# Expert blocks stored by block number, without zeros for the experts' output area

## The chip, the cores and the metric

One core of a Trainium2 chip runs the whole program. The metric is the device time of one execution in microseconds. TensorE (PE), VectorE (DVE), ScalarE (ACT), GpSimd (POOL) and SyncE (SP) each run their own list of instructions; semaphores order them, and SyncE here issues most of the DMA transfers.

## What is computed

16 images of 128 channels and 32 x 32 points go through six layers, each added to what comes in. Only the fourth is touched, a mixture of eight gated experts, of which each token takes the two best:

```python
x = x + conv0(group_norm(x)); x = x + conv1(group_norm(x))
t = tokens(x)                                   # 16 * 1024 tokens of 128
t = t + attention(layer_norm(t))
# the gated mixture
n = layer_norm(t)
vals, idx = top_k(n @ Wg + bg, 2);  w = softmax(vals)
a, g = split(n @ W1[e] + b1[e], 2)              # for each expert e of 8
y[e] = (silu(a) * g) @ W2[e] + b2[e]
t = t + sum_k w[k] * y[idx[k]]
t = t + decay_attention(layer_norm(t));  t = t + second_mixture(layer_norm(t))
```

## The kernel before, in words

The program runs five stages, one after the other, each a block of its own in which every engine has its list; at a block's end all engines meet before the next begins.

1. `convolution_stage` (L80) does both convolution layers. SyncE loads the images and the small weights, waits for the maps of the attention over space (L202 to L208), and then, from L210, issues `FILLS` = 17 transfers that write zeros over the whole of `slots_out`, and one that writes zeros over the last 8 blocks of `slots_in` (L215). At the stage's end TensorE transposes the images and ScalarE copies them into the tile `T` (L468).
2. `attention_stage` (L557) begins with loads of its weights on SyncE's queue (L739 to L743, counted by the semaphore `loaded`, and eight of `Wo` at L749) and with GpSimd's constants (L791 to L807). VectorE waits for the five loads and all constants, then takes the statistics of the first tokens (L914). TensorE's first work is the transposition of the first normalised tokens (L1160). For each image the stage also picks the two experts of each token. A token's row number in `slots_in` is `e * REGION` plus a count, for each of the two; `slots_of` (L1013) keeps the numbers in `route["slots"]`, 128 x 256, and GpSimd writes the normalised tokens to those rows.
3. `experts_stage` (L1295, here with `gated=True`, names with `c_`) walks `MAX_BLOCKS` = 71 blocks of `SLOTS` = 512 rows. VectorE plans first: from the counts in `route["base"]` come the blocks per expert (`full`), their running sum (`ends`), and for each block number its expert and first row (`row_i`). Every expert has a region of 16,896 rows in `slots_in` and `slots_out`, filled from its start. For a block `j` SyncE loads `row_i[j]` into a register and issues the load of its rows (L1408), and for block `j - 5` loads its row again and issues the store of its results to the same rows of `slots_out` (L1413).
4. `decay_stage` gathers the results back: GpSimd reads row numbers from `route["slots"]` and issues gathers from `slots_out` (L2446 to L2454).
5. `mixture_stage` is the last layer.

The work of the experts stage is an order written out by hand. For a block `j`, VectorE runs, in `@block.vector`:

```python
for j in range(MAX_BLOCKS):
    multiply(j, 0)          # L1502: silu(a) * g, first 128 hidden
    if j + 1 < MAX_BLOCKS:
        split_x(j + 1)      # L1495: x - x_hi, the low part of the input
    low(j)                  # L1508: low part of the product
    if j >= 2:
        copy_y(j - 2)       # L1515: results out of PSUM
    multiply(j, 1)          # L1502: second 128 hidden
```

`multiply(j, u)` waits for ScalarE's `first(j, u)` (L1554). ScalarE runs, in this order, `add_bias(j - 2)`, `high(j - 1, 1)` (L1562, which waits for `multiply(j - 1, 1)`), `first(j, 0)`, `high_x(j + 1)`, `high(j, 0)`, `first(j, 1)`. GpSimd copies a block's weights (L1436) and computes the low part of the second product (L1447) once `high(j, 1)` is done. TensorE begins a block with `unit(j, 0)` (L1610 to L1612), which waits for `split_x(j)`; `second(j - 1, 0)`, `turn_x(j + 1)`, `turn_y(j - 2)`, `unit(j, 1)` and `second(j - 1, 1)` follow.

## Time and profile before

| | |
|---|---|
| median of three runs | 4566.6 us (4561.16 to 4569.98) |
| the profiled execution | 4562.08 us, its span 4560.4 us |
| busy share: PE, DVE, ACT, POOL | 82%, 72%, 47%, 42% |
| moved by DMA | 237.52 MB, of it written to HBM 144.31 MB |
| experts stage, blocks | 71, stored by 71 transfers of 256 KB |
| zero fills | 17 of 4096 KB (`slots_out`), one of 2048 KB and eight of 256 KB (`slots_in`) |

Times in the profile are microseconds from the start of the span. A row of a timeline gives the start, the length, the engine, the line of the kernel, the operation and its tiles, the count of merged instructions and, in brackets, how long the engine was idle before and what released it. SPq is SyncE's instruction queue: the length of a DMA row there is the time to issue it, not to move the data. PEclk is the granted clock of TensorE, 1.00 for 2.4 GHz and 0.50 for 1.2 GHz.

### The profile page before, as it was taken

How to read it: one execution, taken by the hardware profiler on the slowest of the kernel's cores; microseconds unless marked ns; L12 is line 12 of the kernel's file. 1: busy time of each engine (PE TensorE's matmuls, PEld its weight loads, DVE VectorE, ACT ScalarE, POOL GpSimd, SP SyncE). 2: the span in 40 equal slices, each digit the busy share in tenths (PEclk: the TensorE clock that was granted, in tenths of full speed). 3: DMA queues.
4: the chain of work that ended last, by engine and by line, in shares of the span. 5: the costliest groups of instructions: out<-in, count | busy, mean ns of one | idle time of the engine just before them, and what ended most of it. 6: DMA issues, size and time to landing. Idle time of an engine off the chain costs nothing. (4 is left out here: it accounts for less than half of the span.)

```text
span 4560.4 us, 74420 instructions
## 1 busy us (share of the span) xinstructions
PE 3719.4 (82%) x21802; PEld 1983.8 (44%) x21802; DVE 3278.3 (72%) x6678; ACT 2140.1 (47%) x3740; POOL 1924.8 (42%) x2046
## 2 busy tenths in 40 slices
PE   1627999989999898999947994488888786999999
PEld 0111222332333332333216883255555555777777
DVE  6737788888888888888815664555556566777777
ACT  1012666666666666666636773122222233444444
POOL 0311033322223323332234553466666653777776
PEclk9976999999999999999978997699999998999999
DMA  2982111121122222222003331000000001000000
GB/s 74 353 302 39 24 30 35 30 37 32 34 36 37 38 37 38 37 37 37 11 23 121 105 105 53 16 30 29 28 28 28 28 19 33 24 23 23 23 23 23
DMA packets 132977, 237.52 MB, mean 52 GB/s; under 512 B 27632, under 2 KB 32952, under 8 KB 132600
## 3 DMA queue, kind: packets, MB, share of 16 engines
q1 hardware_dynamic: 115736, 200.51, 16.4%
q0 software_dynamic: 16384, 33.59, 2.5%
q8 instruction: 134, 2.20, 0.2%
q14 instruction: 147, 1.20, 0.1%
q10 hardware_dynamic: 576, 0.02, 0.0%
HBM read 89.74 MB, written 144.31 MB: 51 GB/s over the span
## 5 line engine op out<-in xcount | busy, mean ns | idle before, releaser
L1143 ACT ACTIVATE b_probs<-b_ps_s 128x512 f32<-128x512 f32 x2048 | 1173.8, 596 | 708.1 <-PE b_ps_s L1187 670.0
L940 DVE TENSOR_REDUCE b_maxes<-b_ps_m 128x1 f32<-128x1024 f32 x1024 | 1215.6, 1214 | 268.7 <-PE b_ps_m L1175 266.0
L1187 PE MATMUL b_ps_s<-b_qs,b_ks 99*128 99x512 bf16 x2048 | 788.9, 390 | 54.8 <-DMA b_ks<-b_k_parts 15.2
L1175 PE MATMUL b_ps_m<-b_ks,b_qs 96*128 96x512 bf16 x2048 | 642.5, 396 | 113.5 <-DVE b_maxes L940 92.0
L1881 POOL TENSOR_TENSOR e_act_lo<-e_act,e_act_hi 128x512 fp32r<-128x512 f32 x384 | 521.8, 1359 | 239.4 <-DVE e_act_hi L1810 239.4
L1199 PE MATMUL b_ps_o<-b_probs,b_vs 128*32 128x512 f32 x4096 | 559.6, 619 | 23.6 <-ACT b_probs L1143 22.8
L1187 PEld LDWEIGHTS b_ps_s<-b_qs,b_ks 99*128 99x128 bf16 x2048 | 199.3, 98 | 845.6 <-ACT b_probs L1143 668.8
L2082 ACT ACTIVATE e_act<-e_ps_h,e_bias 128x512 f32<-128x512 f32 x384 | 264.3, 689 | 411.6 <-PE e_ps_h L2136 290.9
L1985 DVE TENSOR_TENSOR e_act<-e_act,e_ps_g 128x512 f32<-128x512 f32 x384 | 261.5, 681 | 145.9 <-ACT e_act L2082 145.9
L814 POOL TENSOR_TENSOR b_rstd<-b_mv,b_eps 128x8 f32<-128x8 f32 x32 | 6.5, 202 | 744.5 <-DVE b_mv L921 744.5
L1175 PEld LDWEIGHTS b_ps_m<-b_ks,b_qs 96*128 96x128 bf16 x2048 | 188.7, 100 | 301.5 <-DVE b_maxes L940 179.3
L2669 DVE TENSOR_TENSOR d_inner<-d_ps_s,d_decay 128x512 f32<-128x512 f32 x256 | 169.1, 681 | 180.6 <-PE d_ps_s L2951 176.9
L880 POOL DMA_INDIRECT slots_in<-b_xn,b_slot x256 | 248.1, 969 | 97.6 <-issue 81.0
L2450 POOL DMA_INDIRECT d_y<-slots_out,d_slot_now x256 | 247.2, 966 | 88.0 <-issue 71.5
L1810 DVE CAST e_act_hi<-e_act 128x512 fp32r<-128x512 f32 x384 | 244.2, 636 | 0.0
L2134 PE MATMUL e_ps_h<-e_x_hi,e_w_hi 128*128 128x512 f32 x384 | 159.0, 414 | 47.4 <-DVE e_x_lo L1969 42.5
L2826 ACT ACTIVATE d_xn<-tokens,d_shift,d_rstd 128x128 f32 (+1 forms) x256 | 104.9, 482 | 181.4 <-POOL d_shift L2503 181.4
L1502 DVE SCALAR_TENSOR_TENSOR c_act<-c_ps_h,c_bias,c_half_way 128x512 f32<-128x512 f32 x142 | 106.6, 751 | 103.5 <-ACT c_half_way L1554 100.5
L1199 PEld LDWEIGHTS b_ps_o<-b_probs,b_vs 128*32 128x32 f32 x4096 | 81.7, 109 | 206.0 <-issue 141.9
L2685 DVE TENSOR_TENSOR d_state<-d_ps_k,d_block_mask 128x128 f32<-128x128 f32 x224 | 64.2, 287 | 142.4 <-PE d_ps_k L2977 140.6
L853 POOL TENSOR_TENSOR b_taken<-b_hit 128x64 bf16<-128x64 f32 x16 | 5.2, 324 | 380.2 <-DVE b_hit L1001 380.2
L2863 ACT ACTIVATE d_o_chan<-d_ps_o 128x512 f32<-128x512 f32 x64 | 38.2, 597 | 257.8 <-PE d_ps_o L2985 257.8
(434 smaller groups left out, 7415.9 us busy)
## 6 DMA issues: line engine op xcount, KB each, us to landing
slots_out<-nothing SPq DMA_DIRECT2D x17, 4096.0 KB, 29.8
b_qs<-b_q_parts SPq DMA_DIRECT2D x96, 256.0 KB, 9.1
c_xin<-slots_in SPq DMA_DIRECT2D x71, 256.0 KB, 2.6
slots_out<-c_y_out SPq DMA_DIRECT2D x71, 256.0 KB, 2.0
b_q_parts<-b_qparts SPq DMA_DIRECT2D x16, 768.0 KB, 3.6
a_x<-in_x_dram SPq DMA_DIRECT2D x8, 1024.0 KB, 10.2
normalised_t<-d_xT SPq DMA_DIRECT2D x16, 512.0 KB
e_xb<-normalised_t SPq DMA_DIRECT2D x32, 256.0 KB, 2.8
```

Source lines behind the costliest of these rows:

```text
L880: nc.gpsimd.indirect_dma_start(out=slots_in, out_offset=bass.IndirectOffsetOnAxis(ap=slot[:, k * TILES + j:k * TILES + j + 1], axis=0), in ...
L940: nc.vector.tensor_reduce(maxes[:, kv, u:u + 1], ps_m[:, u % 2], AX.X, ALU.max).then_inc(m_free, 1)
L1143: nc.scalar.activation(probs[:, s % PROBS, j * HALF:(j + 1) * HALF], ps_s[:, j % 2], ACT.Exp).then_inc(exp_done, 1)
L1175: last = nc.tensor.matmul(ps_m[:, u % 2, half * HALF:(half + 1) * HALF], qs[0:STACK, buffer, h * PX + qt * P:h * PX + qt * P + P], ks[0:ST ...
L1187: nc.tensor.matmul(ps_s[:, j % 2], ks[0:rows, parity, kv * PX + tt * P:kv * PX + tt * P + P], qs[0:rows, parity, h * PX + half * HALF:h * ...
L1199: last = nc.tensor.matmul(ps_o[32 * j:32 * j + 32, :], vs[:, parity, tt, g // 2, :], probs[:, s % PROBS, j * HALF:(j + 1) * HALF], start=( ...
L1810: copy(act_hi[:, u % ring_a], act_buf[:, u % RING]).then_inc(hi_done, 1)
L1881: nc.gpsimd.tensor_tensor(act_lo[:, u % ring_a], act_buf[:, u % RING], act_hi[:, u % ring_a], ALU.subtract).then_inc(lo_done, 1)
L1985: nc.vector.tensor_tensor(act_buf[:, u % RING], act_buf[:, u % RING], ps_g[:, (u // units_of_gate) % 2], ALU.mult).then_inc(weighed, 1)
L2082: nc.scalar.activation(act_buf[:, u % RING], ps_h[:, u % ring_h, 0], ACT.Gelu, bias=bias[:, bias_column(u, 0)]).then_inc(a_ready, 1)
L2450: nc.gpsimd.indirect_dma_start(out=y[:, i // TILES, i % TILES], out_offset=None, in_=slots_out, in_offset=bass.IndirectOffsetOnAxis(ap=slo ...
L2669: tt(inner[:, c].rearrange("p (j l) -> p j l", j=GH), ps_s[:, :, c * P:(c + 1) * P], decay[:, g * GH:(g + 1) * GH], ALU.mult).then_inc(inn ...
```

## The change

A block's results are stored at the block's number times 512 rows instead of at the rows that its tokens came from. `slots_out` shrinks from 139,264 rows to 36,352, all of which the 71 stores write, and the 17 fills go. Since the row numbers in `route["slots"]` are numbers in `slots_in`, VectorE shifts them for the gather. For each expert, `moved` is the distance from its region's start to its blocks' place, and `jump` the difference of one expert's to the one before; the numbers of expert 0 stay as they are, and seven passes over the 256 columns add `jump[e]` to all numbers from `e * REGION` on. These passes are spread over blocks 8 to 16.

```diff
-            some = FILL_BLOCKS * SLOTS
-            for k in range(FILLS):
-                sp.dma_start(slots_out[k * some:(k + 1) * some].rearrange("(p b t) c -> p b (t c)", p=P, b=FILL_BLOCKS),
-                             nothing[:].rearrange("p (a n) -> p a n", a=1).broadcast_to([P, FILL_BLOCKS, SLOTS])
-                             ).then_inc(cleared, 16)
...
+        moved = sb(pre + "_moved", [P, E])
+        jump = sb(pre + "_jump", [P, E])
+        placed = past[:].rearrange("p j e -> p (j e)")[:, 0:IMAGES * 2 * TILES]
+        beyond = begun[:].rearrange("p j e -> p (j e)")[:, 0:IMAGES * 2 * TILES]
...
-            sp.wait_ge(cleared, 16 * (FILLS + 1))
+            sp.wait_ge(cleared, 16)
...
-                    at = sp.value_load(row_i[0:1, done:done + 1], min_val=0, max_val=SLOT_ROWS - SLOTS)
-                    sp.dma_start(slot_rows(slots_out, at), y_out[:, done % 2]).then_inc(y_sent[done % 2], 16)
+                    sp.dma_start(slot_rows(slots_out, done * SLOTS), y_out[:, done % 2]).then_inc(y_sent[done % 2], 16)
...
+            steps = [0]
+
+            def renumber(ins):
+
+                steps[0] += 1
+                ins.then_inc(renumbered, 1)
+                dve.wait_ge(renumbered, steps[0])
+
+            def block_starts():
+
+                renumber(tt(moved[:], ends[:], full[:], ALU.subtract))
+                renumber(nc.vector.scalar_tensor_tensor(moved[:], moved[:], float(SLOTS), regions[:], ALU.mult,
+                                                        ALU.subtract))
+                renumber(tt(jump[:, 1:E], moved[:, 1:E], moved[:, 0:E - 1], ALU.subtract))
+                renumber(nc.vector.tensor_copy(placed, route["slots"][:]))
+
+            def move_from(e):
+
+                renumber(nc.vector.scalar_tensor_tensor(
+                    beyond, route["slots"][:], float(e * REGION),
+                    jump[:, e:e + 1].broadcast_to([P, IMAGES * 2 * TILES]), ALU.is_ge, ALU.mult))
+                renumber(tt(placed, placed, beyond, ALU.add))
+
             split_x(0)
             for j in range(MAX_BLOCKS):
                 multiply(j, 0)
+                if j == E:
+                    block_starts()
+                if E < j < 2 * E:
+                    move_from(j - E)
+                if j == 2 * E:
+                    nc.vector.tensor_copy(route["slots"][:], placed)
                 if j + 1 < MAX_BLOCKS:
                     split_x(j + 1)
...
-        slots_out = nc.dram_tensor("slots_out", (SLOT_ROWS, C), F32, kind="Internal").ap()
+        slots_out = nc.dram_tensor("slots_out", (MAX_BLOCKS * SLOTS, C), F32, kind="Internal").ap()
```

Three places show how instructions move. The first is SyncE at the end of the convolution stage and the start of the attention stage, before the change:

```order
L207 DMA a_rows<-a_map 32x16x32 x2
L212 DMA slots_out<-nothing 2048x1x512 x17
L215 DMA slots_in<-nothing 1024x1x512
L83 UNCONDITIONAL_BRANCH
L737 UNCONDITIONAL_BRANCH
L739 DMA b_wq<-in_L_attn_Wq_dram 128x128
```

and with it (here and below its own line numbers, which are smaller by 2 to 7 up to L1323, and differ again behind):

```order
L205 DMA a_rows<-a_map 32x16x32 x2
L208 DMA slots_in<-nothing 1024x1x512
L81 UNCONDITIONAL_BRANCH
L730 UNCONDITIONAL_BRANCH
L732 DMA b_wq<-in_L_attn_Wq_dram 128x128
```

The fill of `slots_in` and all loads of the next stage now stand directly behind the loads of `a_rows`. The second place is VectorE in the experts stage, around block 8 and the first half of block 9, with the change; before it the rows L1524 to L1528 and the pass of block 9 are not there, and all others stand in the same order:

```order
L1499 SCALAR_TENSOR_TENSOR c_act<-c_ps_h,c_bias,c_half_way 128x512 x2
L1524 TENSOR_TENSOR c_moved<-c_ends,c_full 128x8
L1525 SCALAR_TENSOR_TENSOR c_moved<-c_moved,c_regions 128x8
L1527 TENSOR_TENSOR c_jump<-c_moved 128x7
L1528 CAST c_past<-route_slots 128x256
L1492 TENSOR_TENSOR c_x_lo<-c_ps_x,c_x_hi 128x512
L1505 TENSOR_TENSOR c_act_lo<-c_act,c_act_hi 128x512
L1512 COPY c_y_out<-c_ps_t 128x512
L1499 SCALAR_TENSOR_TENSOR c_act<-c_ps_h,c_bias,c_half_way 128x512 x2
L1532 SCALAR_TENSOR_TENSOR c_begun<-route_slots,c_jump 128x256
L1535 TENSOR_TENSOR c_past<-c_past,c_begun 128x256
```

The two `c_act` products in a row are `multiply(j - 1, 1)` and `multiply(j, 0)`; the new work is behind the second, ahead of `split_x(j + 1)`. The third place is SyncE in the steady part of the experts stage, one load and one store before:

```order
L1407 TENSOR_LOAD c_row_i
L1407 ISA x2
L1408 ISA
L1408 DMA c_xin<-slots_in 128x512
L1412 TENSOR_LOAD c_row_i
L1412 ISA x2
L1413 ISA
L1413 DMA slots_out<-c_y_out 128x512
```

and with the change:

```order
L1405 TENSOR_LOAD c_row_i
L1405 ISA x2
L1406 ISA
L1406 DMA c_xin<-slots_in 128x512
L1410 DMA slots_out<-c_y_out 128x512
```

The store's register load is gone. The lists of TensorE, ScalarE and GpSimd hold the same instructions in the same order as before.

## Rows read from the trace of the kernel before

**Rows 1.** The page: what the DMA engines moved, in 40 equal slices.

```profile
GB/s 74 353 302 39 24 30 35 30 37 32 34 36 37 38 37 38 37 37 37 11 23 121 105 105 53 16 30 29 28 28 28 28 19 33 24 23 23 23 23 23
```

**Rows 2.** Timeline from 288 to 326 us, all engines (start, length, what).

```profile
288.68 1.08 ACT L468 ACTIVATE tokens<-a_ps_big 128x512 f32 x2 [0.41 <-PE a_ps_big L523]
291.62 10.81 SPq L215 DMA_DIRECT2D slots_in<-nothing  x1
303.74 4.18 SPq L739 DMA_DIRECT2D b_wq<-in_L_attn_Wq_dram  x1
303.75 0.31 POOL L791 MEMSET b_wo<- 128x256 f32 x1 [56.69 <-POOLq L55]
...
309.34 0.29 POOL L807 TENSOR_SCALAR_AFFINE_SELECT b_tri<-b_ones 128x128 bf16<-128x128 bf16 x1
...
311.84 1.24 SPq L743 DMA_DIRECT2D b_bg<-in_L_ffn_bg_dram  x1
...
316.90 1.65 DVE L914 BATCH_NORM_STATS2 b_stats<-tokens 128x6 f32<-128x128 f32 x8 [42.04 <-DMA b_bg<-in_L_ffn_bg_dram]
...
325.23 1.09 PE L1160 MATMUL b_ps_x<-ident,b_xn 128*128 128x128 f32 x4 [36.24 <-POOL b_xn L837]
```

**Rows 3.** Line L1394, the experts' weights of 64 KB: issue (ns) and landing.

```profile
L1394 SPq DMA_DIRECT2D c_w_raw<-in_L_ffn_W_dram x16: 424/432/452, 2390.9 to 2412.8; - x16
...
DMA to landing us min/median/max: 2.3/2.8/3.1
```

**Rows 4.** Windows: length, PE busy, (other engines,) PEclk, DMA share, GB/s.

```profile
2440.00:2780.00 340.00, 340.00 (x1740) 1.00 0.31 103
...
320.00:346.00 26.00, 13.41 (x32) 6.06 (x32) 4.42 (x8) 3.56 (x6) 10.35 (x10) 0.50 0.11 36
...
275.00:290.00 15.00, 10.10 (x77) 7.92 (x75) 0.00 (x0) 10.85 (x20) 0.00 (x0) 1.00 1.03 384
```

**Rows 5.** Timeline of one block of the experts stage, 2443 to 2449 us.

```profile
2443.66 0.75 DVE L1502 SCALAR_TENSOR_TENSOR c_act<-c_ps_h,c_bias,c_half_way 128x512 f32<-128x512 f32 x1 [1.35 <-ACT c_half_way L1554]
...
2444.00 1.30 POOL L1447 TENSOR_TENSOR c_act_lo<-c_act,c_act_hi 128x512 fp32r<-128x512 f32 x1
...
2444.69 0.69 DVE L1495 TENSOR_TENSOR c_x_lo<-c_ps_x,c_x_hi 128x512 fp32r<-128x512 f32 x1 [0.28 <-ACT c_x_hi L1547]
...
2445.30 0.68 DVE L1508 TENSOR_TENSOR c_act_lo<-c_act,c_act_hi 128x512 fp32r<-128x512 f32 x1
...
2445.90 0.68 DVE L1515 COPY c_y_out<-c_ps_t 128x512 f32<-128x512 f32 x1
...
2446.41 0.39 PE L1610 MATMUL c_ps_h<-c_x_hi,c_w_now 128*128 128x512 f32 x1
...
2446.63 0.75 DVE L1502 SCALAR_TENSOR_TENSOR c_act<-c_ps_h,c_bias,c_half_way 128x512 f32<-128x512 f32 x1
...
2447.41 0.62 ACT L1562 CAST c_act_hi<-c_act 128x512 fp32r<-128x512 f32 x1
...
2448.74 0.75 DVE L1502 SCALAR_TENSOR_TENSOR c_act<-c_ps_h,c_bias,c_half_way 128x512 f32<-128x512 f32 x1 [1.36 <-ACT c_half_way L1554]
```

**Rows 6.** Timeline, VectorE's operations nearest to the new ones, two stretches.

```profile
2392.31 1.32 DVE L1473 TENSOR_TENSOR c_ends<-c_ends,c_full 128x1 f32<-128x1 f32 x7
...
247.93 0.42 DVE L399 TENSOR_TENSOR a_pyr<-a_pyr,a_shift 128x256 f32<-128x256 f32 x1
...
249.54 0.29 DVE L409 TENSOR_SCALAR a_pyr<-a_tmp 128x256 f32<-128x256 f32 x1
```

**Rows 7.** Timeline of the convolution stage, VectorE beside GpSimd.

```profile
141.31 1.25 POOL L265 TENSOR_TENSOR a_x<-a_x,a_kept 128x512 f32 x1 [0.73 <-DVE a_kept L371]
...
141.93 1.18 DVE L371 SCALAR_TENSOR_TENSOR a_kept<-a_product,a_spikes 128x512 f32<-128x512 f32 x1 [0.21 <-DVE a_product L365]
```

**Rows 8.** Timeline of the experts stage's end.

```profile
2786.90 0.69 DVE L1515 COPY c_y_out<-c_ps_t 128x512 f32<-128x512 f32 x1 [3.25 <-PE c_ps_t L1631]
...
2788.32 0.33 SPq L1413 DMA_DIRECT2D slots_out<-c_y_out  x1
```

More of the change, by code:

```diff
@@ L28 @@
 SPARE_BLOCKS = E
-FILL_BLOCKS = 16
-FILLS = (E * REGION // SLOTS + SPARE_BLOCKS) // FILL_BLOCKS
 SLOT_ROWS = E * REGION + SPARE_BLOCKS * SLOTS
@@ L77, with convolution_stage @@
 SQUEEZED = 8
-def convolution_stage(nc, T, ident, slots_in, slots_out, nothing, cleared, dram):
+def convolution_stage(nc, T, ident, slots_in, nothing, cleared, dram):
     with ExitStack() as ctx:
@@ L1352, in experts_stage @@
         plan = sem(pre + "_plan")
+        renumbered = sem(pre + "_renumbered")
         padded = sem(pre + "_padded")
@@ L3055, in _ @@
                 pool.wait_ge(ident_zero, 2)
-        convolution_stage(nc, T, ident, slots_in, slots_out, nothing, cleared, dram)
+        convolution_stage(nc, T, ident, slots_in, nothing, cleared, dram)
         gates = sb("gates", [P, TILES * IMAGES * E])
```

## The prediction

> **What bounds the kernel now.** I read the page by 40 slices first. In slices 2 and 3 the DMA engines move 353 and 302 GB/s, ten times what they move through most of the rest [rows 1]: these are the 17 zero fills that the change removes, 4096 KB each. So the first question is whether anything waited for them. The list of waits around the end of the convolution stage says that VectorE did, 42.0 us until the load of `b_bg` landed, and that GpSimd waited 56.7 us for its release at the stage's end [rows 2].
>
> The timeline of that stretch shows the order of events [rows 2]. ScalarE's last work of the convolution ends at 288.68 + 1.08 = 289.76. SyncE is then still issuing: the last fill of `slots_out` holds it until 291.62 and the fill of `slots_in`, which comes behind, until 302.43. Only then does the stage end for all; GpSimd starts at 303.75, 1.32 us later. The loads of the attention stage stand behind the fills in the same queue: the issue of `b_wq` takes 4.18 us and that of the fifth load 1.24, and VectorE, which waits for all five, starts at 316.90. The nearest issues in a queue with little in it, weights of the experts, take 0.43 us and land in 2.3 to 3.1 us [rows 3]. Before 289.76 the list of waits has no engine that waits for a fill.
>
> The other end of the change lies in the experts stage. There TensorE is busy 340.00 of 340.00 us, at a granted clock of 1.00 [rows 4], one block every 5.08 us (the DVE row L1502 of `multiply(j, 0)` comes at 2443.66 and 2448.74 [rows 5]). VectorE works about two thirds of that time, and idles 1.36 us just before `multiply(j, 0)` and 0.28 before `split_x` [rows 5].
>
> **The fills removed.** SyncE now reaches the 2048 KB fill of `slots_in` some 165 us before the stage's end. So ScalarE ends the stage: 289.76 + 1.32 = 291.08 is GpSimd's start. Two things must then be ready for VectorE. GpSimd's constants take from 303.75 to 309.34 + 0.29 = 309.63, that is 5.88 us, so they are ready at 296.96. SyncE's five loads take 5 x 0.43 = 2.2 us to issue and up to 3.1 to land, ready at 296.4. The constants are the later by a little; with 0.1 for the semaphore VectorE starts at 297.1 and not at 316.90: **19.8 us earlier**, and all behind it moves as one piece. The eight `b_wo` loads behind the five are issued by some 4 us later, before 298, and TensorE wants them at its first transposes, 325.23 - 19.8 = 305.4 [rows 2]: hidden. `slots_out` needs no zeros for anyone else: a gathered row is always one that a block stored.
>
> **VectorE's new work in the experts stage.** 19 instructions, all between `multiply(j, 0)` and `split_x(j + 1)`, each but the last waited for before the next: in block 8 three on 8 columns and a cast of 256; in blocks 9 to 15 two on 128x256; in block 16 a cast of 256. Prices [rows 6]: seven linked operations on one column take 1.32, so 0.20 each with the wait; 128x256 with two inputs in SBUF 0.42; 256 columns with one input in SBUF 0.29. I take 0.42 + 0.03 for each of the large ones, the cast among them, so 0.90 for a pair; 0.29 + 0.03 is the lower bound.
>
> Does 0.90 fit in? The idle time says so (1.36 + 0.28 = 1.64 a block), but the order does not. From one `multiply(j, 0)` to the next runs a chain without TensorE, by the durations and starts in rows 5: `multiply(j, 0)` 0.75, `split_x` 0.61, `low` 0.60, `copy_y` 0.68, from `multiply(j, 1)` to ScalarE's `high(j, 1)` 0.78, from there over `first(j + 1, 0)` to `multiply(j + 1, 0)` 1.33. That is 4.75, under TensorE's 5.08; with the pair it is 5.65, so each of seven blocks goes 0.57 us slower than TensorE could: 4.0 us. It shows as TensorE waiting for `x_lo` at the start of a block.
>
> Block 8 comes first, and there the lag that TensorE can bear counts. `x_lo` is ready at 2444.69 + 0.69 = 2445.38 and used at 2446.41: 1.03 to spare [rows 5]. The inserted work would start at 2444.41, while GpSimd's L1447, which reads two tiles in SBUF, runs from 2444.00 to 2445.30. Such a meeting is in the trace: beside L265, VectorE's L371, of 512 columns with two inputs in SBUF, takes 1.18, where L1508 of that kind and size takes 0.68 alone, and it ends 0.55 after L265 does [rows 5, 7]. So the first small operation gets going at 2445.30, the cast ends at 2445.30 + 3 x 0.20 + 0.45 = 2446.35, `split_x` at 2447.04, and TensorE loses 0.63. Without the meeting `x_lo` would come at 2446.15 and leave 0.26 to spare: the stage would lose 4.0 - 0.26 = 3.7 and not 4.6. From block 9 on the two stay apart: `high(j - 1, 1)` ends 0.71 before `multiply(j, 0)` starts and releases L1447, whose 1.30 end at +0.59, and the pair starts at +0.75.
>
> The Trainium skill (SBUF — State Buffer, section Who interferes with whom) says of this meeting that a VectorE instruction with two SBUF inputs and a GpSimd instruction that reads SBUF take a shared port in turn, the later one fully blocked; the trace agrees, with the 1.18 beside 0.68. With that rule in block 8 the stage loses 4.6, without it 3.7; if it struck in all of blocks 9 to 15 too, the upper bound below would hold.
>
> In block 16 the cast makes the chain 5.20: 0.1. **Together 4.7 us lost**, between 1 (a pair of 0.64, a chain of 5.39, 0.31 a block, less the 1.03 that TensorE bears) and 13 (each of eight blocks also waits out a GpSimd operation of 1.30, on top of 4.0, less what TensorE bears).
>
> **SyncE in the experts stage.** A store no longer loads its row number. TensorE is never idle in the steady part, so 70 of 71 are worth nothing. The last one is on the path: VectorE's copy ends at 2786.90 + 0.69 = 2787.59 and the store is issued at 2788.32 [rows 8], ahead of the stage's end. The 0.73 between shrinks to about 0.1: **0.6 us gained**. The gather of the next stage keeps its instructions, and only the rows that it reads lie elsewhere: nothing.
>
> **The sum.** -19.8 + 4.7 - 0.6 = -15.7 us. The profiled execution took 4562.08 us (its span is 4560.4), which gives 4546.4. It stands 4.5 below the median of the three runs, 4566.6, with which a new median compares: 4566.6 - 15.7 = 4550.9, say **4551**.
>
> **Rivals.**
> 1. *The clock stays up.* From 320 to 346 TensorE is busy 13.41 us at a granted clock of 0.50, that is 1.2 GHz [rows 4], mostly in a chain where one engine waits for the next. If the shorter gap kept the clock at 2.4 GHz, half of that would go, 6.7 us more: 4544. Against it: the gap is still 305.4 - 289 = 16 us. Chance 0.07.
> The Trainium skill (TensorE: Matmul & The Clock Gate, section What's actually happening) calls the low clock the default, which activity has to lift; by it the clock is down at 305 as well and the sum stays.
> 2. *The loads are slow by themselves.* If 4.18 + 4 x 1.24 = 9.1 belongs to these transfers and not to the full queue, `b_bg` is issued by 300.2 and lands some 3.8 later (316.90 less 311.84 + 1.24), VectorE starts at 304.1, the first term is 12.8 and the sum -8.7: 4558. Against it: the weights of the experts, issued in 0.43 [rows 3]. Chance 0.12, half of it within 0.2% of before.
> 3. *The new work costs nothing*, because the chain is looser than its starts say: -20.4, 4546. It lies inside the forecast's bounds.
> 4. *Slower.* TensorE stalls in each of blocks 8 to 16; if the stalls made its clock fall to 1.2 GHz there, a block would last about twice 5.08, and nine blocks would lose 9 x 5.1 = 46 us: net -15.7 + 46, 30 us slower, 4597. It decides from the point where the stalls leave TensorE so idle that the clock falls. Against it: from 275 to 290 it was busy 10.10 of 15.00 us and was granted 1.00 [rows 4], and a stall of 0.6 in 5.7 leaves it far busier. Chance 0.04.
> 5. *The change does not free the stage's end*, since something that the waits do not show holds it as long. Then nothing measurable changes. Chance 0.03.
>
> **How the numbers follow.** The forecast has 0.74. Its own range is 4545 to 4559: the experts stage between 1 and 13 gives 4547 to 4559, and 2 go to the spread of medians (the three runs lie 8.8 apart). With rivals 1 and 2 taken in, 4541 to 4560 leaves out under 2 in 10. A difference of 0.2%, 9.1 us, is what a measurement of this kernel can tell from none: faster 0.74 + 0.07 + 0.06 = 0.87, same 0.06 + 0.03 = 0.09, slower 0.04.
>
> **What would show it.** Right: VectorE's first row of the attention stage near 297, `b_wq` issued in about 0.4 near 291, DMA slices 2 and 3 nearly empty; in blocks 9 to 15 of the experts stage starts of `multiply(j, 0)` 5.6 to 5.7 apart, with TensorE waiting for `x_lo`. Wrong: a start later than 300; blocks still 5.08 apart, or 6 and more; a granted clock below 1.00 there; or an attention stage whose length from VectorE's start is another than before.

## The result, and the profile after

| | before | after |
|---|---|---|
| median, first comparison | 4569.98 us (4561.16 to 4576.64, 5 runs) | 4547.56 us (4545.13 to 4553.67, 5 runs) |
| median, second comparison | 4566.91 us (4562.39 to 4571.95, 15 runs) | 4551.57 us (4547.03 to 4557.52, 5 runs) |
| ratio with its 95% interval | | 0.9953 (0.9940 to 0.9967), then 0.9965 (0.9951 to 0.9979) |
| the profiled execution, its span | 4562.08, 4560.4 us | 4547.56, 4545.8 us |
| written to HBM | 144.31 MB | 73.01 MB |

The change is faster by 22.4 us in one comparison and by 15.3 in the other, about 0.4% of the time. The profiled pair differs by 14.5; the prediction's sum was 15.7.

The fills are gone from slices 2 and 3, which had 353 and 302 GB/s [rows 1]. The page after:

```profile
GB/s 74 21 26 29 27 37 31 29 30 33 35 32 36 38 37 38 37 37 37 11 43 109 105 103 49 16 31 29 28 28 28 28 19 33 24 23 23 23 23 24
```

Timeline of the changed kernel from 288 to 305 us, the stretch of [rows 2]:

```profile
288.06 1.09 ACT L461 ACTIVATE tokens<-a_ps_big 128x512 f32 x2 [0.41 <-PE a_ps_big L516]
290.06 0.36 SPq L732 DMA_DIRECT2D b_wq<-in_L_attn_Wq_dram  x1
290.07 0.31 POOL L784 MEMSET b_wo<- 128x256 f32 x1 [43.27 <-POOLq L53]
...
291.92 0.43 SPq L736 DMA_DIRECT2D b_bg<-in_L_ffn_bg_dram  x1
...
295.66 0.29 POOL L800 TENSOR_SCALAR_AFFINE_SELECT b_tri<-b_ones 128x128 bf16<-128x128 bf16 x1
296.06 1.64 DVE L907 BATCH_NORM_STATS2 b_stats<-tokens 128x6 f32<-128x128 f32 x8 [21.46 <-POOL b_tri L800]
...
304.39 1.08 PE L1153 MATMUL b_ps_x<-ident,b_xn 128*128 128x128 f32 x4 [16.03 <-POOL b_xn L830]
```

ScalarE now ends the stage, at 289.15, and GpSimd starts 0.92 later. The five loads are issued in 0.36 to 0.46 us each where `b_wq` took 4.18 and `b_bg` 1.24. What releases VectorE has changed from the load of `b_bg` to GpSimd's last constant. It starts at 296.06 and not at 316.90, 20.84 us earlier, and TensorE's first transposition is 20.84 earlier too.

In the experts stage the new work has a price. Timeline of the changed kernel, blocks 8 and 9, VectorE, GpSimd and two matmuls of TensorE:

```profile
2446.28 0.75 DVE L1499 SCALAR_TENSOR_TENSOR c_act<-c_ps_h,c_bias,c_half_way 128x512 f32<-128x512 f32 x1 [1.35 <-ACT c_half_way L1580]
2446.63 1.29 POOL L1444 TENSOR_TENSOR c_act_lo<-c_act,c_act_hi 128x512 fp32r<-128x512 f32 x1
2446.95 1.00 DVE L1524 TENSOR_TENSOR c_moved<-c_ends,c_full 128x8 f32<-128x8 f32 x1
...
2448.71 0.69 DVE L1492 TENSOR_TENSOR c_x_lo<-c_ps_x,c_x_hi 128x512 fp32r<-128x512 f32 x1
...
2452.00 1.28 POOL L1444 TENSOR_TENSOR c_act_lo<-c_act,c_act_hi 128x512 fp32r<-128x512 f32 x1 [0.24 <-ACT c_act_hi L1588]
...
2452.54 0.75 DVE L1499 SCALAR_TENSOR_TENSOR c_act<-c_ps_h,c_bias,c_half_way 128x512 f32<-128x512 f32 x1 [1.28 <-ACT c_half_way L1580]
2453.21 0.41 DVE L1532 SCALAR_TENSOR_TENSOR c_begun<-route_slots,c_jump 128x256 f32<-128x256 uint32 x1
2453.66 0.42 DVE L1535 TENSOR_TENSOR c_past<-c_past,c_begun 128x256 f32<-128x256 f32 x1
2454.12 0.69 DVE L1492 TENSOR_TENSOR c_x_lo<-c_ps_x,c_x_hi 128x512 fp32r<-128x512 f32 x1
...
2454.44 0.40 PE L1650 MATMUL c_ps_y<-c_act_hi,c_w_now 128*128 128x512 f32 x1
2454.91 0.47 PE L1636 MATMUL c_ps_h<-c_x_hi,c_w_now 128*128 128x512 f32 x1
...
2455.93 0.74 DVE L1499 SCALAR_TENSOR_TENSOR c_act<-c_ps_h,c_bias,c_half_way 128x512 f32<-128x512 f32 x1
2457.95 0.75 DVE L1499 SCALAR_TENSOR_TENSOR c_act<-c_ps_h,c_bias,c_half_way 128x512 f32<-128x512 f32 x1 [1.28 <-ACT c_half_way L1580]
```

Block 8 lasts 6.26 us from one first multiply to the next, blocks 9 to 15 last 5.40 each (2452.54 to 2457.95 is the first), blocks 16 and 17 last 4.69 and 4.84. TensorE now waits for VectorE's `x_lo` where a pass stands ahead of it: its first matmul of block 10 (L1636) starts 0.47 behind the matmul ahead of it, where 0.23 is usual, and 0.10 behind the end of `split_x` at 2454.81. Windows of the changed kernel (length, busy time of PE, its weight loads, DVE, ACT and POOL, then PEclk, DMA share, GB/s) show that TensorE is no longer busy without a gap, and that its clock is up in the experts stage:

```profile
293.00:296.00 3.00, 0.00 (x0) 0.00 (x0) 0.00 (x0) 0.00 (x0) 2.81 (x7) 0.50 0.10 18
320.00:326.00 6.00, 4.08 (x17) 3.48 (x16) 1.09 (x2) 0.97 (x2) 1.45 (x2) 0.50 0.16 33
2440.00:2500.00 60.00, 59.15 (x294) 46.78 (x293) 43.59 (x75) 42.09 (x68) 32.91 (x35) 1.00 0.30 101
```

From block 8's first multiply to block 26's it takes 94.36 us, in both executions of the kernel before 91.44; from block 26's to block 70's it takes 224.16, before 223.60. That is 2.9 and 0.6, **3.5 us** in all. The experts stage begins with a row of GpSimd; in the kernel before, and in the changed one:

```profile
2390.55 0.21 POOL L1419 IOTA c_number<- 128x71 f32 x1 [4.95 <-POOLq L55]
```

```profile
2373.41 0.21 POOL L1416 IOTA c_number<- 128x71 f32 x1 [4.95 <-POOLq L53]
```

The sum for the profiled pair: -20.84 at VectorE's first statistics of the attention stage; +3.70 from there to this row, though the attention stage has no edit (2073.65 us before, 2077.35 after); +2.24 from this row to GpSimd's first row of the next stage (the 3.5, less 0.7 for the earlier last store and 0.5 by which the stage's first block was shorter, 4.89 for 5.41, which varies from execution to execution: it took 4.90 in the second execution of the kernel before); +0.38 behind it. Together -14.52. The 3.70 do not belong to the change: the kernel before, executed once more, took 2077.32 for the same stretch (its row is shown with that run).

### The profile page after: what moved, and what is told of

Same layout as the page of the kernel before. It is cut to its first block and busy times, and to the rows that moved or that the text cites. A ratio compares the mean times of both kernels' runs of the same rounds, so it can differ in the third digit from the quotient of the medians.

```text
span 4545.8 us, 74075 instructions
## 1 busy us (share of the span) xinstructions
PE 3720.9 (82%) x21802; PEld 1984.2 (44%) x21802; DVE 3286.6 (72%) x6697; ACT 2140.7 (47%) x3740; POOL 1926.0 (42%) x2046
## 3 DMA queue, kind: packets, MB, share of 16 engines
HBM read 89.74 MB, written 73.01 MB: 36 GB/s over the span
```

## The experiments

### The start: how many fills can stay

The kernels leave the storage by block number as it is and put fills back, into an area that nothing reads: `FILLS` = 17 as before (the diff), and 12 and 16 in two more.

```diff
+            unused = nc.dram_tensor("unused", (SLOT_ROWS, C), F32, kind="Internal").ap()
+            some = FILL_BLOCKS * SLOTS
+            for k in range(FILLS):
+                sp.dma_start(unused[k * some:(k + 1) * some].rearrange("(p b t) c -> p b (t c)", p=P, b=FILL_BLOCKS),
...
-            sp.wait_ge(cleared, 16)
+            sp.wait_ge(cleared, 16 * (FILLS + 1))
```

> The changed kernel, but the 17 fills stay, into an area of the old size that nobody reads; the sixth-stage work and the stores by block number stay as changed. Theory (SyncE ends the convolution stage and its queue delays the loads): VectorE starts the attention stage at 316.9 again, 20.8 us later than in the changed kernel, and the convolution up to ScalarE's last copy is as long as before; the experts stage still loses its 3.5 us, so the total is 2 to 4 us over the kernel before, apart from the attention stage's own spread. Rival (the smaller results area itself speeds up something, or the fills slow the convolution's work): a start between 297 and 316.

> As the one before, with 12 of the 17 fills, 71% of the bytes. Theory: at 10.9 us a fill they end near 122 + 12 x 10.9 = 253, well ahead of ScalarE's last copy at 289, so the attention stage starts at 296 as in the changed kernel: all of the 20.8 us gained with 29% of the fills gone. Rival (bytes that compete with the stage's work): 29% of the gain, a start near 311.

> The same with 16 of 17 fills. Theory: the queue is free 10.9 us earlier than with 17, so GpSimd is released at 303.7 - 10.9 = 292.9 and VectorE starts at 316.9 - 10.9 = 306.0: half of the whole gain for one fill. Rival (bytes): a seventeenth of it, a start near 315.7.

> The changed kernel once more, for the spread of the attention stage. Theory: the positions of its start (296.1), the block spacing of 5.40 in blocks 9 to 15 of the experts stage and the 3.5 us lost there repeat within 0.2 us; the attention stage does not: its images last 119.5 to 123.5 us by the dips of TensorE's granted clock that fall into them, and their sum moves by 2 to 5 us. Rival (the attention stage is longer or shorter by something systematic of the change): the same image lengths as in the first profile.

Timeline of the kernel with 17 fills:

```profile
288.05 1.08 ACT L469 ACTIVATE tokens<-a_ps_big 128x512 f32 x2 [0.41 <-PE a_ps_big L524]
292.46 10.10 SPq L216 DMA_DIRECT2D slots_in<-nothing  x1
303.86 4.01 SPq L740 DMA_DIRECT2D b_wq<-in_L_attn_Wq_dram  x1
...
316.82 1.64 DVE L915 BATCH_NORM_STATS2 b_stats<-tokens 128x6 f32<-128x128 f32 x8 [42.16 <-DMA b_bg<-in_L_ffn_bg_dram]
```

Timeline of the kernel with 16:

```profile
281.10 11.62 SPq L216 DMA_DIRECT2D slots_in<-nothing  x1
294.03 4.25 SPq L740 DMA_DIRECT2D b_wq<-in_L_attn_Wq_dram  x1
...
306.72 1.64 DVE L915 BATCH_NORM_STATS2 b_stats<-tokens 128x6 f32<-128x128 f32 x8 [31.37 <-DMA b_bg<-in_L_ffn_bg_dram]
```

And with 12:

```profile
290.82 0.37 SPq L740 DMA_DIRECT2D b_wq<-in_L_attn_Wq_dram  x1
...
296.83 1.64 DVE L915 BATCH_NORM_STATS2 b_stats<-tokens 128x6 f32<-128x128 f32 x8 [21.83 <-POOL b_tri L808]
```

With the fills alone back, the start is back to 316.82 (316.90 in the kernel before, 316.53 in its second execution). With 16 the forecast was 306.0, with 12 it was 296. The seventeenth is worth 10.1 us, the four before it 9.9 together, about as much as one; with twelve all of the gain is there and the constants release VectorE (the 0.77 against 296.06 is a later last copy of ScalarE, 289.90 for 289.15). So the start's 20.8 belong to the fills alone, and at least twelve of the 17 held nobody; 13 to 15 weren't tried. With 12 fills the loads are issued in 0.37 to 0.50, with 16 in 4.25 and 1.24: the slow issue belongs to the fills that the queue still holds and not to these loads, which settles rival 2. The whole times of these two, one execution each, are 4558.54 with 16 fills and 4556.92 with 12. The second is 10 us below the kernel before and not 20: its last two stages, which have no edit, took 1777.5 us from GpSimd's first row on, where the other executions lie between 1768.1 and 1773.0. So the rows carry this argument, not the totals.

The kernel with 17 fills takes 4570.8 us against 4566.91, ratio 1.0011 (1.0001 to 1.0020, that is 0.5 to 9 us): with the gain taken away, the storage by block number costs about 4 us, barely clear of nothing; the rows account for 2.8 of them, 3.5 less 0.7 for the earlier last store. The second execution of the changed kernel has its blocks as the first (94.38, and 6.26, 5.40 for block 8 and 9 to 15) and starts the statistics at 296.39; from its first exponentials to its last the attention stage is 6.4 us longer, more than the 2 to 5 expected.

One plain rival of the whole change was not tried: the fills removed and the old storage kept. The plan gives each expert as many blocks as its tokens fill, rounded up, and stores all of them, so every row that the gather reads is written in the old storage too. By the rows this would gain the start's 20.8 us without new work of VectorE, at the price of the larger `slots_out`; no run shows it.

### The experts stage: where the passes stand

Four kernels move or multiply the passes within a block. The first puts them behind `multiply(j, 1)`, the second issues the comparing operation three times in place, the third gives every second block a pass, the fourth puts them behind `low(j)`. Their diffs follow in this order; in the last one, too, the six lines are gone from behind `multiply(j, 0)`.

```diff
                 multiply(j, 0)
-                if j == E:
-                    block_starts()
-                if E < j < 2 * E:
-                    move_from(j - E)
-                if j == 2 * E:
-                    nc.vector.tensor_copy(route["slots"][:], placed)
...
                 multiply(j, 1)
+                if j == E:
+                    block_starts()
+                if E < j < 2 * E:
+                    move_from(j - E)
+                if j == 2 * E:
+                    nc.vector.tensor_copy(route["slots"][:], placed)
```

```diff
-                renumber(nc.vector.scalar_tensor_tensor(
...
+                for _ in range(3):
+                    renumber(nc.vector.scalar_tensor_tensor(
```

```diff
-                if E < j < 2 * E:
-                    move_from(j - E)
-                if j == 2 * E:
+                if E < j <= 3 * E - 2 and (j - E) % 2 == 0:
+                    move_from((j - E) // 2)
+                if j == 3 * E:
```

```diff
                 low(j)
+                if j == E:
+                    block_starts()
+                if E < j < 2 * E:
+                    move_from(j - E)
+                if j == 2 * E:
+                    nc.vector.tensor_copy(route["slots"][:], placed)
                 if j >= 2:
                     copy_y(j - 2)
```

> The passes over the row numbers stand behind the second multiply of their block instead of behind the first. In the changed kernel VectorE waits 1.35 us there in an undisturbed block (1.28 between two passes), and a pass is 0.91 us (0.45 and 0.46 from start to start). Theory (a chain of operations inside one block that is 5.40 us long against TensorE's 5.08): the passes of blocks 9 to 15 cost nothing and the first multiplies of these blocks stand 5.08 to 5.10 us apart; block 8 costs 0 to 0.5, by what its first small operation meets on GpSimd. The stage is then 2.3 to 3.0 us shorter than in the changed kernel. Rival (each pass has a price by itself, through the port, the semaphores or the instruction stream, wherever it stands): the blocks stay near 5.40 and the stage as long as it is.

> The comparing operation of each pass is issued three times instead of once, with the same result: two more operations of 0.45 us from start to start in each of the blocks 9 to 15. Theory of the chain: the whole of it comes on top, the first multiplies stand 5.40 + 0.90 = 6.30 us apart in seven blocks, and the stage is 6.3 us longer than in the changed kernel. Rival (VectorE's idle time in a block, 1.28 us, takes the passes in and what was lost is something else): less than 0.3 us of each 0.90 shows, the stage grows by under 2 us.

> One pass in every second block (10, 12 to 22), the cast back in block 24. In the changed kernel the two blocks behind the last pass are 4.69 and 4.84 us long, 0.63 under the usual 5.08 together: VectorE catches up when it may. Theory of the chain (4.49 us without a pass, 5.40 with one, TensorE's 5.08 between): a block with a pass is 5.3 to 5.4 long and the one behind it 4.7 to 4.8, so that seven passes cost nothing together; what is left is block 8's, 1.18 less about 0.6 regained. The stage is 2 to 2.5 us shorter than in the changed kernel. Rival (a fixed price of 0.32 per pass): the blocks in between stay at 5.08 and the stage is as long as in the changed kernel within 0.3 us.

> All operations on the row numbers stand behind the subtraction of the low parts of the product instead of ahead of the subtraction that makes the low parts of the next block's input. Theory 1 (two conditions: TensorE's next block waits for the low parts of its input, so only what stands ahead of that operation is on the chain; and an operation whose operands all lie in SBUF waits for the end of GpSimd's operation when the two meet): in an undisturbed block of the changed kernel GpSimd is idle from 1.64 to 3.87 us behind the first multiply, and this place begins 2.27 behind it, so that a pass of 0.91 meets nothing and delays only the copy of the output and the second multiply, which have 1.35 us of room. Blocks 8 to 16 are 5.08 to 5.10 us long, the operations take 0.42 and 0.43 (0.16 for the first small one), the stage is 2.5 to 3 us shorter than in the changed kernel. Rival (what the run with the passes last showed is general: a pass costs more the later it stands, because the second multiply or the copy gates the following block): the blocks are above 5.40. Third (a pass costs 0.3 wherever it meets nothing): they stay at 5.40.

| kernel | blocks with a pass, us | block 8's first multiply to block 26's | whole time |
|---|---|---|---|
| before | none (5.08) | 91.44 | 4566.91 to 4570.47 (medians) |
| after | 5.40 | 94.36 | 4547.56, 4551.57 (medians) |
| comparing operation three times | 6.32 | 100.80 | 4562.37 (one execution) |
| every second block | 6.02, the one behind it 4.66 | 95.75 | 4553.58 (one) |
| behind `low(j)` | 5.58 | 94.67 | 4547.90 (one) |
| behind `multiply(j, 1)` | 6.14 | 99.59 | 4553.09 (one) |
| in VectorE's wait (below) | none (5.095) | 91.68 | 4545.56 (median) |

Executions of one kernel lie 10 to 16 us apart, so the single times decide nothing here; the stretch of the third column repeats within 0.02 us wherever a kernel was executed twice.

**Three times: as expected.** 6.32 is 5.40 + 0.92, all of it on top. VectorE's idle time of 1.28 us a block hides nothing of it.

**Behind the second multiply: my theory fell.** It should have been free, since VectorE is idle there, and it was the dearest. Timeline of that kernel, block 11:

```profile
2466.72 0.74 DVE L1499 SCALAR_TENSOR_TENSOR c_act<-c_ps_h,c_bias,c_half_way 128x512 f32<-128x512 f32 x1
...
2467.00 1.47 POOL L1433 CAST c_w_now<-c_w_all 128x1536 fp32r x1
...
2467.38 1.37 DVE L1532 SCALAR_TENSOR_TENSOR c_begun<-route_slots,c_jump 128x256 f32<-128x256 uint32 x1
...
2468.43 1.47 POOL L1444 TENSOR_TENSOR c_act_lo<-c_act,c_act_hi 128x512 fp32r<-128x512 f32 x1
...
2468.78 1.41 DVE L1535 TENSOR_TENSOR c_past<-c_past,c_begun 128x256 f32<-128x256 f32 x1
```

Each of the two operations meets one of GpSimd's and ends 0.28 and 0.29 behind its end: 1.37 and 1.41 us for what takes 0.41 and 0.42 alone. The next first multiply follows at 2470.22, right behind the pass: the 1.35 us of idle time are used up and more. VectorE is idle at this place in the very time in which GpSimd works. The Trainium skill (SBUF — State Buffer, section Who interferes with whom) says that an exclusive lock on a shared pair of ports decides this, and the one that comes second is fully blocked; the rows agree, with 1.37 beside 0.41. What has one input in PSUM is spared: `split_x` takes 0.69 beside GpSimd's subtraction in [rows 5].

**Every second block: also not free.** I had counted on 5.3 to 5.4 for a block with a pass and 4.7 to 4.8 for the one behind it, and on a stage 2 to 2.5 us shorter than the changed kernel's. Timeline of that kernel, block 10:

```profile
2460.08 0.75 DVE L1499 SCALAR_TENSOR_TENSOR c_act<-c_ps_h,c_bias,c_half_way 128x512 f32<-128x512 f32 x1 [1.27 <-ACT c_half_way L1580]
2460.23 1.30 POOL L1444 TENSOR_TENSOR c_act_lo<-c_act,c_act_hi 128x512 fp32r<-128x512 f32 x1
2460.75 1.06 DVE L1532 SCALAR_TENSOR_TENSOR c_begun<-route_slots,c_jump 128x256 f32<-128x256 uint32 x1
```

Here L1444 starts 0.15 behind the first multiply and not 0.54 ahead of it, as in block 9 of the changed kernel. Behind a block without a pass GpSimd's operation comes that late, and the first operation of the pass waits out L1444: 1.06 for 0.41, and 1.03 to 1.06 in all seven. Passes in consecutive blocks shift VectorE against GpSimd and thereby keep clear of it; single ones meet it each time. The spread placement costs 1.4 us more than the dense one.

**Behind `low(j)`: no meeting, and still not free.** Timeline, block 9 of that kernel:

```profile
2450.16 0.75 DVE L1499 SCALAR_TENSOR_TENSOR c_act<-c_ps_h,c_bias,c_half_way 128x512 f32<-128x512 f32 x1 [1.27 <-ACT c_half_way L1580]
2450.82 0.68 DVE L1492 TENSOR_TENSOR c_x_lo<-c_ps_x,c_x_hi 128x512 fp32r<-128x512 f32 x1
2450.94 0.62 ACT L1588 CAST c_act_hi<-c_act 128x512 fp32r<-128x512 f32 x1 [0.33 <-DVE c_act L1499]
2451.59 0.69 DVE L1505 TENSOR_TENSOR c_act_lo<-c_act,c_act_hi 128x512 fp32r<-128x512 f32 x1
2452.21 0.41 DVE L1532 SCALAR_TENSOR_TENSOR c_begun<-route_slots,c_jump 128x256 f32<-128x256 uint32 x1
2452.66 0.43 DVE L1535 TENSOR_TENSOR c_past<-c_past,c_begun 128x256 f32<-128x256 f32 x1
...
2453.72 0.74 DVE L1499 SCALAR_TENSOR_TENSOR c_act<-c_ps_h,c_bias,c_half_way 128x512 f32<-128x512 f32 x1
...
2455.74 0.75 DVE L1499 SCALAR_TENSOR_TENSOR c_act<-c_ps_h,c_bias,c_half_way 128x512 f32<-128x512 f32 x1 [1.28 <-ACT c_half_way L1580]
```

The expectation took only what stands ahead of `split_x` for the chain. The prediction had it right and I had dropped it: the next first multiply follows the second one through ScalarE, whose list has `high(j, 1)` ahead of `first(j + 1, 0)`. From 2453.72 to 2455.74 is 2.02, and it is 2.02 in the changed kernel too (2455.93 to 2457.95). So all that VectorE does between its two multiplies is on the chain: 3.56 + 2.02 = 5.58. It is 0.18 more than in front, because `low(j)` waits for ScalarE's `high(j, 0)`, which ends at 2451.56, and a pass in front of it fills that wait. The kernel with every second block shows the same wait in a block without a pass: there `low(j)` starts 0.77 behind `split_x` and not 0.60, and the block lasts 4.66.

The changed kernel's own order is thus the best of the four inside the loop that were tried, and none of the four is free: between the two multiplies the chain is the limit, behind the second the shared port. The places behind `split_x` and behind `copy_y` weren't tried; they lie between the two multiplies, on the same chain.

### Out of the loop, and a better start

At the stage's start VectorE waits 9.08 us for the weights of expert 3, the fourth one (`e == 3`; the two expectations below call it the third). The next kernel does all the new work there; the one after it also takes the statistics of the attention stage's first image ahead of VectorE's wait for the weights and constants. In both the six lines behind `multiply(j, 0)` are gone.

```diff
             for e in range(E):
+                if e == 3:
+                    block_starts()
+                    for later in range(1, E):
+                        move_from(later)
+                    nc.vector.tensor_copy(route["slots"][:], placed)
...
-                if isinstance(n, int) and n < 0:
-                    statistics(0, 0, 0)
-                    statistics(0, 0, 1)
...
+            statistics(0, 0, 0)
+            statistics(0, 0, 1)
             dve.wait_ge(loaded, 16 * 5)
             dve.wait_ge(const, 11)
```

> All operations on the row numbers (about 7.5 us of VectorE's time) stand ahead of the third expert's weights at the start of the experts stage, where VectorE waits some 9 us for a transfer; none is left in the blocks. Theory: no block is longer than in the kernel before (5.08 to 5.10 us each), the experts stage gives back the 3.5 us that the change added there, the start gain of 20.8 us stays, and the time is 3 to 4 us under the changed kernel's, some 4544 to 4549 us, 0.995 to 0.996 of the kernel before. Rival (the passes cost where they stand: the first blocks' weights come late, or the gather of the numbers isn't ready): the first multiply of the stage is 2 us or more later behind the stage's start than in the changed kernel and the time is not lower.

> The operations on the row numbers in VectorE's wait at the start of the experts stage, and the statistics of the attention stage's first image ahead of VectorE's wait for the weights and GpSimd's constants. In the changed kernel the last copy of the first stage ends at 289.1, the statistics start at 296.1, 0.1 behind GpSimd's last constant, and take 2.6 with the means. Theory: they now run from about 289.5 on and GpSimd's first step on them follows its last constant at about 296.0 instead of 298.7: the attention stage starts 2.6 us earlier, and the time is 2 to 3 us below the kernel with the operations in the wait alone, 4542 to 4546. Rival (the first normalisation waits for a weight's transfer or something else of the start): the first transposition on TensorE stays where it is, at 304 us, and the time is that of the kernel with the operations in the wait, 4545 to 4549.

Timeline of the first, the start of the experts stage:

```profile
2389.61 0.16 DVE L1493 TENSOR_TENSOR c_moved<-c_ends,c_full 128x8 f32<-128x8 f32 x1
...
2396.97 0.29 DVE L1511 CAST route_slots<-c_past 128x256 uint32<-128x256 f32 x1
...
2398.69 0.69 DVE L1514 TENSOR_TENSOR c_w_all<-c_w_raw,c_w_all 128x512 fp32r<-128x512 f32 x1 [1.43 <-ACT c_w_all L1560]
```

The work takes 7.65 us and 1.43 of the wait is left. The blocks are 5.09 and 5.10 us long, 91.68 for the stretch: of the 2.9 us there 2.7 are back, and 0.24 are not. The median is 4545.56 us (4538.79 to 4555.00, 6 runs) against 4569.90, ratio 0.9946 (0.9932 to 0.9959), in the expected range. The interval overlaps both of the changed kernel's (0.9953 and 0.9965), so that it is faster than the changed kernel is shown by the rows and not by the whole time.

Timeline of the second, the start of the attention stage:

```profile
289.97 1.65 DVE L907 BATCH_NORM_STATS2 b_stats<-tokens 128x6 f32<-128x128 f32 x8 [15.42 <-PEq L53]
...
296.02 0.20 POOL L807 TENSOR_TENSOR b_rstd<-b_mv,b_eps 128x8 f32<-128x8 f32 x1 [0.21 <-POOL b_tri L800]
...
301.75 1.08 PE L1152 MATMUL b_ps_x<-ident,b_xn 128*128 128x128 f32 x4 [13.53 <-POOL b_xn L830]
```

The first transposition comes at 301.75 and not at 304.39, 2.64 earlier. The median is **4538.60 us** (4535.91 to 4542.85, 5 runs) against 4568.96, ratio **0.9933** (0.9919 to 0.9947), 30 us below the kernel before. It is the lowest median here, and below the 4542 to 4546 that were expected. The rows account for 2.6 + 2.7 us below the changed kernel, whose medians are 9.0 and 13.0 higher; the rest has no row and lies within what executions differ by.

### Two things left

> The kernel before once more, to see what belongs to it and what to one execution. Theory (the attention stage's length, from its first exponentials to its last, goes with how long TensorE's granted clock was at the lower level in it: 1914 to 1915 us with 75 to 89 us at that level, 1919 to 1921 with 89 to 99): 1910 to 1922 us, by that sum, and not by the kernel; the blocks of the experts stage are 5.08 us long each and the statistics start at 316.8 to 317.6. Rival (the two kernels have attention stages of different length, 1913.9 against 1918 on the mean): 1913 to 1915 again.

> The kernel with the operations in VectorE's wait and the early statistics, and in it SyncE loads a block's row number into its register once more between its wait for the results and the issue of the store, as the kernel before does, without using it. What is asked: in all kernels with the new storage a block of the experts stage where nothing stands is 5.095 us long (44 blocks take 224.15), in both executions of the kernel before 5.082 (223.60), also where no operation on the row numbers is left in the blocks. In them the store is issued 2.98 us behind the first multiply of a block and the load of a block's rows 4.07 behind it, in the kernel before 3.66 and 4.79. Theory (the earlier transfers of the store meet TensorE's or another engine's accesses): with the register load back the two issues stand where they stood and the 44 blocks take 223.6, the stage 0.8 us less in all; in the whole time it doesn't show, 4536 to 4541. Rival (it is something else of the kernel, the stored rows' places or the layout of its instructions): 224.1 to 224.2 again.

The kernel before starts its statistics at 316.53 this time (316.8 to 317.6 was expected), and the experts stage with

```profile
2393.84 0.21 POOL L1419 IOTA c_number<- 128x71 f32 x1 [4.95 <-POOLq L55]
```

That is 2077.32 us for the attention stage, where its first execution took 2073.65 and the changed kernel 2077.35: the 3.70 us that the profiled pair lost there is what the kernel before differs by from itself. Only 0.9 of the 3.7 lie between the first exponentials and the last, 1.3 ahead of them and 1.5 behind.

From its first exponentials to its last the stage took 1913.9 and 1914.9 us in the two executions of the kernel before, as the rival said, and between 1911.1 and 1921.2 in twelve of kernels with the new storage, 1916.3 on the mean. It goes loosely with how long TensorE's clock was granted at the lower level in short stretches of it: 71.7 us of it with 1911.1, 75.1 with 1914.8, 78.5 with 1914.9, 81.9 with 1913.9 and 1915.2, 85.3 with 1912.7 to 1918.8, 88.7 with 1914.9 to 1920.1, 99.0 with 1921.2. Up to 6 us of difference stand beside one and the same sum, so the clock explains a part at most, and which of the two causes the other isn't shown. Whether the new storage makes this stretch some 2 us longer stays open, with two executions of the kernel before.

The undisturbed block is 5.095 us long in all twelve profiled executions with the new storage, and 5.082 in both before. Most of the difference stands in one step of TensorE, from the first matmul of a set of three (L1636) to the second (L1637; L1610 and L1611 before), four times a block: 0.2555 us on the mean of blocks 30 to 67 in the changed kernel, 0.2524 before. The other steps differ by up to 0.003 either way and nearly cancel. For the last run SyncE loaded the row number again ahead of each store, without use:

```diff
                     sp.wait_ge(y_copied, done + 1)
+                    sp.value_load(row_i[0:1, done:done + 1], min_val=0, max_val=SLOT_ROWS - SLOTS)
                     sp.dma_start(slot_rows(slots_out, done * SLOTS), y_out[:, done % 2])
```

Timeline of that kernel:

```profile
2601.82 0.75 DVE L1527 SCALAR_TENSOR_TENSOR c_act<-c_ps_h,c_bias,c_half_way 128x512 f32<-128x512 f32 x1 [1.35 <-ACT c_half_way L1579]
...
2605.36 0.33 SPq L1410 DMA_DIRECT2D slots_out<-c_y_out  x1
```

The store is 3.54 us behind the first multiply, 3.66 in the kernel before and 2.98 in the changed one, and the 44 blocks take 224.14: the theory of the earlier store falls. What makes a block 0.013 us longer, 0.8 us in all, stays open; the places of the stored rows and the layout of the instructions weren't varied by themselves. The median of this kernel, 4542.77 us (4536.81 to 4549.83, 4 runs), lies above the expected 4536 to 4541; its ratio, 0.9943 (0.9926 to 0.9960), is not apart from that of the kernel without the load.

## Why the prediction was right

Forecast 4551, measured 4547.56 and 4551.57; the profiled sum -15.7 against -14.5. The two mechanisms, the start held by the fills and the longer chain in the blocks with a pass, came as told. That the numbers meet so closely is in part luck. What the rows give to the change itself is -20.2 at the start, +3.5 in the blocks and -0.7 at the last store, -17.4 together, between the -15.3 and the -22.4 of the two comparisons. In the profiled pair the attention stage added 3.7, which are no effect of the change, and the experts stage's first block and ScalarE's end took away 0.5 and 0.6. The prediction had named an attention stage of another length as a sign of being wrong; it came, and the second execution of the kernel before shows that such a length varies without any change. Step by step:

- **The fills removed, -19.8: -20.84.** The order of events was as told: ScalarE ends the stage, the loads are issued in 0.4, the constants come last, and the first row of the stage is released by `b_tri`. The sum was 1.0 short: 0.4 because the release takes 0.92 and not the 1.32 of [rows 2], and 0.6 because ScalarE's last copy ends at 289.15 and not at 289.76. That end lies between 288.8 and 290.1 in all executions, whatever fills there are (289.13 with 17 of them, 289.15 in the second execution of the kernel before), so this 0.6 is no effect of the fills.
- **The new work, +4.7: +2.7.** This is the term that was mis-sized. The mechanism held: the chain over both multiplies and ScalarE, the meeting in block 8 (1.00 us for an operation that takes 0.16 alone), none in blocks 9 to 15. The pair was 0.91 for 0.90. But the rest of the chain is 4.49 us and not 4.75, so a block with the pair lasts 5.40 and loses 0.31 to 0.32, not 0.57. Two steps were taken as durations though an operation starts before the one ahead of it ends when it is ready: `multiply(j, 0)` to the next operation is 0.67 (0.75 taken), `copy_y` to `multiply(j, 1)` 0.60 (0.68 taken). The third came from a block in which TensorE sets the pace, so that it held idle time: from `multiply(j, 1)` to the next first multiply it is 2.02 (2.11 taken). A block without a pass can't run in 4.49 all the same: `low(j)` then waits for `high(j, 0)`, a step that the prediction's chain lacked, and the shortest blocks last 4.66. So of the pair's 0.91 only 0.74 came on top. The cast of block 16 cost nothing: 4.69 for the 5.20 forecast. Block 8 lost 1.17 in VectorE's starts (6.26 for 5.09), of which blocks 16 and 17 gave 0.66 back: 0.5, for 0.63.
- **Unforeseen, +0.8:** the 0.013 us of each undisturbed block.
- **The last store, -0.6: -0.7.** The wait between VectorE's last copy and SyncE's issue was 0.73; now the copy ends at 2773.37 and the store is issued at 2773.40.
- **The rivals.** The clock was not up at the start (0.50 from 320 to 326 us, and TensorE is without work from 293 to 296), and it did not fall in the experts stage (1.00). The loads weren't slow by themselves. The new work wasn't free. Of the two rules of the Trainium skill, that of the low clock as the default (TensorE: Matmul & The Clock Gate, section What's actually happening) went the way in which it was used, with 0.50 granted behind the gap. So did that of the lock (SBUF — State Buffer, section Who interferes with whom): block 8 shows it, and the run with the passes last at a price of 0.74 us per block more than in the loop's front.

## What to carry to other kernels

A transfer that nobody reads can still be dear through the queue: look at what stands behind it in the issuing engine's list at a stage's end, and how many of such transfers it takes before anyone waits; here at least twelve of seventeen were free and the last one alone cost 10 us. An engine's idle time is no offer of room. Follow the loop's chain from an operation to itself one turn later, with starts, not durations, from a block in which the chain and not another engine sets the pace, and look at what the neighbour on the shared port does in the gap; work that no block needs goes to a long wait outside the loop.

## What the runs showed of the hardware

- VectorE and GpSimd: an operation of VectorE with all its operands in SBUF, 128 x 256, that starts beside a GpSimd operation reading SBUF takes 1.03 to 1.41 us for 0.41, and ends 0.28 to 0.29 behind GpSimd's end; one on 128 x 8 takes 1.00 for 0.16 and ends 0.03 behind it. It met a GpSimd cast as it met a subtraction. GpSimd's subtraction took 1.47 for 1.29 where it started beside the end of VectorE's operation (2468.43 in the run with the passes last).
- SyncE's queue: with 16 or 17 fills of 4 MB ahead, the fill of 2 MB holds SyncE 10 to 12 us, the next small load 4.0 to 4.3 and each further one 1.24; with 12 ahead each takes 0.37 to 0.50.
- TensorE's granted clock was at the 1.2 GHz level for 72 to 99 us of the attention stage, in 20 to 26 short stretches with 2.4 GHz between, while the engine was some 91% busy (1719 of 1884 us in the execution with the least), and at other places in every execution. The stretch from the first exponentials to the last differed by up to 10 us between executions of kernels that are the same there, loosely with these sums.
